# Two multi-head attentions of a gated cross-attention network: loops unrolled, each projection split one and three matmuls, queries and norms on ScalarE

## The reference, cut to what matters

```
scores = q @ k.T            # per head, 256 x 256
w      = softmax(scores)    # A2: masked keys at a huge negative value
heads  = w @ v              # 256 x 16 per head
out    = concat(heads) @ Wo
```

## Time and profile before

| | us |
|---|---|
| runs shown, median (lowest to highest) | 3025.44 (3023.05 to 3033.63) |
| profiled execution, its own time | 3053.3 |
| its span, first to last instruction | 3051.6 |
| MHA window, 190 to 965 us | 775 |
| A2 window, 1778 to 2165 us | 387 |

### The profile page before, as it was taken

How to read it: one execution, slowest core, us unless ns; L and a number is a source line. 1 busy time by engine, 2 the same in 40 slices (tenths; PEclk the granted TensorE clock), 3 DMA queues, 4 the chain that set the end, 5 groups by cost and what they waited for, 6 DMA issues and landing times. The chain is left out here.

```text
span 3051.6 us, 56496 instructions
## 1 busy us (share of the span) xinstructions
PE 2722.6 (89%) x19773; PEld 2165.8 (71%) x19774; DVE 1743.8 (57%) x4748; ACT 1143.3 (37%) x2188; POOL 627.0 (21%) x1027
## 2 busy tenths in 40 slices
PE   7978999989897899899899778888799998978998
PEld 6855666666665788787787645555588887877998
DVE  5757777777775111688675468888422217861111
ACT  1224444444443221454334424444333324452221
POOL 1211212121221000110464511111011104551111
PEclk9989999999998899999789979999799999988999
DMA  9610000000000443670214311000111102025553
GB/s 324 262 33 2 1 1 1 1 1 1 1 1 2 154 152 134 245 285 11 96 69 133 112 52 30 22 22 15 65 56 55 44 12 77 15 93 184 180 181 120
DMA packets 136169, 247.47 MB, mean 81 GB/s; under 512 B 26716, under 2 KB 86364, under 8 KB 129632
## 3 DMA queue, kind: packets, MB, share of 16 engines
q1 hardware_dynamic: 114608, 185.11, 18.0%
q10 hardware_dynamic: 11536, 35.28, 3.0%
q0 software_dynamic: 9888, 25.38, 2.3%
HBM read 148.75 MB, written 97.75 MB: 81 GB/s over the span
## 5 line engine op out<-in xcount | busy, mean ns | idle before, releaser
L564 ACT ACTIVATE m0hpT<-banks 128x1024 f32<-128x1024 f32 x256 | 262.9, 1027 | 415.3 <-PE banks L501 413.8
L539 DVE TENSOR_REDUCE m0hnm<-banks 128x4 f32<-128x1024 f32 x256 | 312.0, 1219 | 158.4 <-PE banks L488 156.9
L488 PE MATMUL banks<-m0hk,m0hq 32*128 32x256 f32 x2048 | 294.9, 406 | 71.4 <-DVE m0hnm L539 69.6
L501 PE MATMUL banks<-m0hq,m0hk 32*128 32x256 f32 x2048 | 294.3, 404 | 1.4 <-ACT m0hpT L564 1.4
L488 PEld LDWEIGHTS banks<-m0hk,m0hq 32*128 32x128 f32 x2048 | 177.4, 187 | 165.0 <-DVE m0hnm L539 142.4
L562 ACT ACTIVATE a2hpT<-banks,a2hlow 128x512 f32<-128x512 f32 x256 | 162.2, 684 | 208.0 <-PE banks L501 208.0
L539 DVE TENSOR_REDUCE a2hnm<-banks 128x4 f32<-128x1024 f32 x128 | 156.5, 1223 | 73.7 <-PE banks L488 73.6
L488 PE MATMUL banks<-a2hk,a2hq 32*128 32x256 f32 x1024 | 148.1, 407 | 44.6 <-DVE a2hnm L539 44.6
L501 PEld LDWEIGHTS banks<-m0hq,m0hk 32*128 32x128 f32 x2048 | 179.7, 186 | 3.2 <-issue 1.5
L488 PEld LDWEIGHTS banks<-a2hk,a2hq 32*128 32x128 f32 x1024 | 88.9, 187 | 98.0 <-DVE a2hnm L539 80.5
L3252 PEld LDWEIGHTS banks<-E3xT,E3w 128*128 128x128 f32 x1248 | 147.3, 194 | 2.4 <-DVE E3xT L3176 0.5
(11 more groups left out here) (492 smaller groups left out, 6219.9 us busy)
## 6 DMA issues: line engine op xcount, KB each, us to landing
E3w<-in_L_ffn_W_dram SPq DMA_DIRECT2D x39, 1024.0 KB, 4.8
slots<-A0pad SPq DMA_DIRECT2D x8, 4290.0 KB, 34.2
slots_x<-A1pad ACTq DMA_DIRECT2D x8, 4290.0 KB, 14.3
E0w<-in_L_ffn_fw_dram SPq DMA_DIRECT2D x64, 512.0 KB
E2w<-in_L_ffn_w_dram SPq DMA_DIRECT2D x16, 1024.0 KB
E1xin<-slots SPq DMA_DIRECT2D x71, 130.0 KB
m0hq<-m0hnmT SPq DMA_DIRECT2D x512, 1.0 KB
A2routed<-routed SPq DMA_DIRECT2D x16, 512.0 KB, 3.6
```

The costliest lines, as they stand in the source:

```text
L488: ins = pe.matmul(self.scores[:, j, tc], self.q[strip(half, j), u, e, c, chunk(tc)], self.k[strip(half, j), u, e, c], start=True, stop=True)
L501: ins = pe.matmul(self.turned[:, j, kc], self.k[strip(half, j), u2, e2, c2, chunk(kc)], self.q[strip(half, j), u2, e2, c2], start=True, st ...
L539: v.tensor_reduce(self.nm[:, e, :, at:at + 9:8].rearrange("p c g -> p g c"), self.scores, AX.X, ALU.max, negate=True).then_inc(self.nm_rdy, 1)
L564: ins = a.activation(dst, self.turned, ACT.Exp)
```

## The change

All loops in the two stages go: every batch is written out, with plain integer numbers. PE's order becomes

```diff
+    def tensor(self, pe, n, one=None, rest=None):
+
+        if self.has(n):
+            self.score(pe, n, 0)
+        if self.has(n - 2):
+            self.score_turned(pe, n - 2, 1)
+        if self.has(n - 3):
+            self.weighted(pe, n - 3)
+        if one:
+            one()
+        if self.has(n):
+            self.score(pe, n, 1)
+        if self.has(n - 2):
+            self.score_turned(pe, n - 2, 0)
+        if rest:
+            rest()
```

and a projection comes in two pieces, where one() is the first of four matmuls:

```diff
+def parted(pe, out, lhsT, rhs, ready, sem, after=None):
+
+
+    order = [(m, k) for m in range(C) for k in range(C)]
+
+    def step(m, k):
+        return pe.matmul(out(m), lhsT(k, m), rhs(k), start=(k == 0), stop=(k == C - 1))
+
+    def one():
+        ready()
+        step(*order[0])
+
+    def rest():
+        for m, k in order[1:]:
+            ins = step(m, k)
+        ins.then_inc(sem, 1)
+        if after:
+            after()
+    return one, rest
```

In MHA each of the eight units has one product; the output product is cut by token chunk, 4 matmuls in unit 4 and 4 in unit 7, and goes to bank 5 instead of bank 7:

```diff
+                    hd.tensor(pe, 8 * b, *make_v(0, ready0, after0))
+                    hd.tensor(pe, 8 * b + 1, *make_qk(wq, 1, G0, q_mm, ready1))
+                    hd.tensor(pe, 8 * b + 2, *make_qk(wk, 1, G1, k_mm, ready2))
+                    hd.tensor(pe, 8 * b + 3, *make_v(1, ready3, after3))
...
+                    hd.tensor(pe, 8 * b + 4, *sum_out(b - 1, 0, ready4, after4))
...
+                    hd.tensor(pe, 8 * b + 5, *make_qk(wq, 0, G0, q_mm, ready5))
+                    hd.tensor(pe, 8 * b + 6, *make_qk(wk, 0, G1, k_mm, ready6))
...
+                    hd.tensor(pe, 8 * b + 7, *sum_out(b - 1, 1, lambda: None, after7))
```

Layer norms: POOL computes from one set of statistics both roots (for the doubled norm by algebra) and a shift, and ACT applies them; the copy keep goes, and POOL recomputes the normalised input for the base with two more tensor_scalar:

```diff
+            def norm1(b):
+                r = b % 4
+                g.wait_ge(st1_rdy, b + 1)
+                g.tensor_scalar(var1[:, r, 1], mv1[:, r, :, 1], 1.0 + 1e-6, 1e-11, ALU.mult, ALU.add)
+                ch1.link(g.tensor_tensor(var1[:, r, 0], mv1[:, r, :, 1], env.eps5[:], ALU.add))
+                ch1.link(g.tensor_tensor(root1[:, r].rearrange("p t c -> p (t c)"), var1[:, r].rearrange("p t c -> p (t c)"),
+                                         env.mhalf[:, 0:2 * C], ALU.pow))
+                for c in range(C):
+                    ins = g.tensor_scalar(shift1[:, r, c:c + 1], mv1[:, r, c, 0:1], root1[:, r, 1, c:c + 1], -1.0,
+                                          ALU.mult, ALU.mult)
+                ins.then_inc(rstd1_rdy, 1)
...
+            def take_q(job, e):
+                a.wait_ge(q_mm, job + 1)
+                for c in range(C):
+                    ins = a.activation(hd.q[:, job % 2, e, c], G0[:, c], ACT.Identity, bias=bqe[:, job % 2, e, c:c + 1],
+                                       scale=hd.column(2 + e))
+                if e == 1:
+                    ins.then_inc(hd.q_rdy, 1)
+
...
+            def apply1(b):
+                a.wait_ge(rstd1_rdy, b + 1)
+                if b:
+                    a.wait_ge(n1_mm, b)
+                for c in range(C):
+                    ins = a.activation(nn1[:, c], env.x[:, b, c], ACT.Identity, scale=root1[:, b % 4, 1, c:c + 1],
+                                       bias=shift1[:, b % 4, c:c + 1])
+                ins.then_inc(nn1_rdy, 1)
```

```diff
+            def add_routed(b):
+
+                g.wait_ge(high_in[b % 2], 16 * (b // 2 + 1))
+                g.tensor_tensor(env.x[:, b], env.x[:, b], routed[:, b % 2, :, 0:D], ALU.add).then_inc(high_add, 1)
+                g.wait_ge(high_add, b + 1)
+                g.tensor_tensor(env.x[:, b], env.x[:, b], routed[:, b % 2, :, D:2 * D], ALU.add).then_inc(low_add, 1)
...
+            def add_bias(b):
+
+                g.wait_ge(xn_rdy, b + 1)
+                g.tensor_tensor(env.x[:, b], env.x[:, b], bp[:].unsqueeze(1).broadcast_to([P, C, D]), ALU.add).then_inc(bias_rdy, 1)
...
+            def finish(b):
+                v.wait_ge(bias_rdy, b + 1)
                 v.wait_ge(y_mm, b + 1)
-                v.tensor_tensor(y[:], G1, bp[:].unsqueeze(1).broadcast_to([P, C, D]), ALU.add).then_inc(y_rdy, 1)
-
-            def finish(b):
-                v.wait_ge(y_rdy, b + 1)
-                v.scalar_tensor_tensor(env.x[:, b], y[:], env.tg[:, 2:3], env.x[:, b], ALU.mult, ALU.add)
-
-            ch.start(0)
...
+                def pre3():
                     if more:
+                        take_k(b + 1, 0)
...
+                hd.tensor(pe, 4 * b, one0, rest0)
+                if more:
+                    hd.tensor(pe, 4 * b + 1, *make_q(b + 1, ready1))
+                    hd.tensor(pe, 4 * b + 2, *make_k(b + 1, ready2))
+                    hd.tensor(pe, 4 * b + 3, *make_v(b + 1, ready3))
```

More of the change, by code:

```diff
@@ L532, in vector, with has @@
-    def vector(self, v, job, u, i, first, mid=None, end=None):
-        new = self.parts(i, first)[0]
-        n, _, c, e = self.unit(job, u, i)
-        def highest(half):
-            v.wait_ge(self.s_mm, 2 * n + half + 1)
-            at = 16 * half
-            v.tensor_reduce(self.nm[:, e, :, at:at + 9:8].rearrange("p c g -> p g c"), self.scores, AX.X, ALU.max,
-                            negate=True).then_inc(self.nm_rdy, 1)
-        if new:
-            highest(0)
+    def has(self, n):
+        return 0 <= n < self.units
@@ new lines, in weighted @@
+    def weighted(self, pe, n):
+        u, c, e = self.place(n)
+        if n % 4 == 0:
+            pe.wait_ge(self.v_rdy, n // 4 + 1)
+        if e == 0 and n:
+            pe.wait_ge(self.raw_rdy, n // 2)
+        pe.wait_ge(self.p_rdy, 2 * n + 2)
+        for kc in range(C):
+            for g in range(4):
+                ins = pe.matmul(self.out[32 * g:32 * g + 32, e], self.v[:, u, kc, 8 * c + 2 * g + e],
+                                self.pT[:, e, g, kc], start=(kc == 0), stop=(kc == C - 1), tile_position=(0, 32 * g))
+        ins.then_inc(self.av_mm, 1)
@@ L953, in _, with rows_of @@
         @block.scalar
         def _(a):
-            def turned(mm, count, bank, dst, gain, bias, sums, done, at):
+            def rows_of(mm, count, dst, gain, bias, sums, done, at):
                 a.wait_ge(mm, count)
@@ L2272, in job @@
-            def job(b, u, first, last):
-                start, more = first and u == 0, not (last and u == 1)
-                ch.start(b + 2)
+            first_stats(0)
+            last_stats(0)
+            take_k(0, 0)
+            take_k(0, 1)
+            first_stats(1)
+            last_stats(1)
+            add_flags(1, 5).then_inc(low_rdy, 1)
+            v.wait_ge(low_rdy, 2)
+            v.wait_ge(hd.made, 3)
+            for b in range(B + 2):
+                more = b + 1 < B
                 def end0():
-                    if not start:
+                    if within(b - 1):
@@ L2386, in _ @@
+            one()
+            rest()
             turn(0, G1)
-            pe.wait_ge(q_in, 16)
-            make_q(0)
-            pe.wait_ge(w_in, 16 * loads)
-            make_v(0)
-            def job(b, u, first, last):
-                start, more = first and u == 0, not (last and u == 1)
-                def fill0():
+            pe.wait_ge(xnT_rdy, 1)
+            one, rest = make_q(0, lambda: pe.wait_ge(q_in, 16))
+            one()
+            rest()
+            pe.wait_ge(hd.q_rdy, 1)
```

1088 lines of the change are left out of this document (509 added, 579 removed).

## The result

The changed kernel takes 2914.36 us, median of 4 runs (2908.54 to 2917.27), the one before 3024.24 (3022.89 to 3033.63) on the same chip: a ratio of 0.9628, 95% interval 0.9603 to 0.9653. The profiled execution took 2908.5 us, its span 2906.7.

The account below looks back on a forecast made before the run. No engine full; order bounds: PE and DVE take turns in phase A (half 0 to half 1), PE sets phase B (the rest of a unit). MHA 67 and A2 33 us, together 100 off 3025.4: 2925 us, range 2880 to 2975.

Parts of the forecast that it names:

- Unit: One group of heads with two maxima: PE's work 2.63 us in phase A, 2.55 in phase B, together 5.18.
- Turns and logits: Extra PE work in MHA, two of each per batch, four at 0.50 us on top of eight units.
- DVE's lateness: MHA maxima held up: 0.3 us a batch by DVE's own work plus 0.4 by POOL, 0.7 in all.
- The collision of DVE and POOL: MHA unit 3's residual add, both inputs in SBUF, beside POOL's base: 0 to 0.9 us a batch, taken as 0.4.
- The rival of 2983 us: DVE's two-input adds wait up to 1.27 us behind POOL, six places, 58 us more in all; chance 0.12.
- DVE gives work away: Per MHA batch DVE loses four query takes and all normalisation applications; the second statistics go altogether.
- A2's batch: Units of 5.8, 5.18, 5.18 and 5.75 us, sum 21.9, saving 2.1 a batch; unit 3's maximum 0.6 late.
- The rival of code loading: Straight-line PE code must stream, from 5 us per former loop pass; at 6 us the time is 3045; chance 0.04.
- Start and tail: MHA starts 2 us earlier; its tail ends 2 to 3 later, as batch 14's second norm moves behind the last scores.
- Full drains: Rival: each unit's two new shape changes cost 0.14 us more, 27 us over 192 units: 2952; chance 0.15.
- Overlap: Rival: PE's shape changes overlap, the unit falls to 5.0 us, 35 us more gained: 2890; chance 0.12.
- no change: Rival: the single matmul delays half 1 as much as phase B shortens, DVE stays late: 3025; chance 0.03.

Follow-up runs that it names:

- experiment 1: Changed kernel with the single matmul put back, products whole behind half 1's scores, MHA's output product still halved: 2952.52 us, ratio 0.9765.
- experiment 2: Changed kernel with queries and norm applications back on DVE in both stages, PE's new order kept: 2944.32 us, ratio 0.9732.
- experiment 5: Changed kernel with MHA's output product in one piece in unit 4, none in unit 7: 2941.80 us, ratio 0.9732.
- experiment 6: Changed kernel with A2's two adds of routed rows on DVE again instead of POOL: 2934.30 us, ratio 0.9686.
- experiment 8: Changed kernel with the single matmul ahead of the weighted sums instead of behind them: 2918.82 us, ratio 0.9655.
- experiment 10: Changed kernel with four parts undone at once, those of experiments 1, 2, 5 and 6: 2997.66 us, ratio 0.9908.
- experiment 3: Changed kernel with the edits of experiments 1 and 2 together: 2978.97 us, ratio 0.9839.
- experiment 11: Kernel of experiment 10 with A2's last statistics and residual also back behind unit 1's second maximum: 3007.95 us, ratio 0.9936.
- experiment 4: Kernel before the change with its loops over batches written out, nothing else: 3024.62 us, ratio 0.9988.
- experiment 9: Changed kernel with router's logits in phase A and the product whole behind half 1, in MHA units 0 and 7: 2920.10 us, ratio 0.9634.

## Why the prediction was right, step by step

**The time and the cause** held: PE's gaps in phase A and its surplus in phase B, both set by DVE, are gone, and the two stages are 112 us shorter, against 100 forecast. PE's new order alone carries a third of it (experiment 1), DVE's relief, the halved output product and A2's adds the larger part (experiments 2, 5 and 6), and some 20 us are placed in no part. What each part brought came out otherwise than the terms had it.

**Unit, 5.18 forecast, 5.30 measured.** The mis-sized term is the single matmul. I took a record's step as the mean over a whole product, (1.99 - 0.38)/7 = 0.23 us. The first step of a group is 0.32 and the others 0.215, so the mean holds for no part of it: two records cost 0.62 instead of 0.54, six 1.49 instead of 1.46 us (experiment 8). The step from weighted sums to the full shape, which no row showed and for which I took 0.31, came out as taken (1.01 against 1.00). A plain unit then was said to fall from 5.56 to 5.18; experiment 1 shows 5.48 to 5.30. The split fills a gap of 0.37 us (5.48 - 5.11, the sum of PE's work unsplit) and costs 0.19 (5.30 - 5.11). A third of the gain, where my unit gave it over half.

**Turns and logits, 2.0 a batch forecast, 1.56 measured.** Behind a product they need no change of shape: by the phases 0.34, 0.50, 0.37, 0.34. **DVE's lateness, 0.7 forecast, about 0.1 measured** (units 2 and 6: 5.35 and 5.36). The three errors cancel: 8 x 5.30 + 1.56 + 0.1 = 44.06, for 44.1 forecast. That agreement is luck.

**The collision of DVE and POOL, 0.4 a batch, did not come in the changed kernel.** The residual and POOL's first operation of the base, in the trace of the changed kernel:

```profile
510.49 2.09 POOL L738 TENSOR_SCALAR M0shift<-M0bo,M0probs 128x256 f32<-128x256 f32 x2
```

```profile
511.08 0.71 DVE L801 SCALAR_TENSOR_TENSOR x_all<-M0x,tg,x_all 128x512 f32<-128x512 f32 x1
```

DVE's addition with both inputs in SBUF followed its transposition without a gap and ran inside POOL's pair, in 0.71 us. By the Trainium skill's rule that I weighed (SBUF — State Buffer, Who interferes with whom) DVE would have waited for the end of POOL's operation; this row does not show that. POOL's pair took 2.09 us, where it took 1.83 in experiment 10. The rival of 2983 us falls for this kernel. But the rival had a true core, in another place: DVE's norm from SBUF to SBUF took 2.25 us beside both of POOL's additions in experiment 3, and 1.17 us where it overlapped only the first. By giving the norms to ACT the change took that operation off DVE.

**ACT's cost nothing** held: its exponentials are released by PE. **DVE gives work away** had no number of its own; experiment 2 gives 30 us in the median and, of 22 in the profile, 21 in MHA. **A2's batch** was 21.9 for 21.82, by compensation: units 1 and 2 took 5.37 and 5.62 instead of 5.18, unit 3 5.06 instead of 5.75. The key take makes a maximum 0.3 late, not 0.6, which the timeline puts at the end of unit 2, and the following phase A recovers 0.24 of it. The part that I had named in a clause (adds, statistics and finish behind one maximum) is the largest of A2: experiments 6 and 11.

**Unrolling** cost nothing: over the whole of MHA's batch 1 there are 4 instruction packets on that queue in both kernels (the 3 of the earlier trace rows leave out the batch's first 0.2 us), PE has no idle time there that is put down to issue, and experiment 4 finds 0.9988. The rival of code loading falls. **Start and tail:** the first maximum came 2.5 us earlier (forecast 2), but it moves by as much from run to run (188.0 and 190.6 us with the same MHA code); from the last maximum to the last pick 33.1 us instead of 32.9, not 2 to 3 longer. **Full drains** (2952) put 0.14 on a unit; 0.12 was measured, but from the second record on. So in size that rival was nearly right on the unit; what I had priced too dear elsewhere made up for it. The Trainium skill (TensorEngine Tiling (Array Packing), Key Properties) says that a change of tiling mode drains the engine; the runs put the price of one more change at 0.19 us (experiments 1 and 9), and whether a drain is what takes it none of them shows. **Overlap** (2890) and **no change** fall with the same rows.

## What to carry over

Two engines that take turns on the same banks waste the difference of their phases; a split of a product pays only if the gap that it fills (0.37 us here) is wider than the change of shape that it adds (0.19), and so one matmul ahead pays where two do not. Small work on the pacing engine is priced by place: 1.4 us in a middle slot of its own cost nothing, in a slot with other work 0.45, and 1.0 to 1.4 us behind a maximum 0.6 to 0.8. A record is priced by its position in its group and not by the group's mean. And parts are undone both alone and together: the output product and the adds were worth 27 and 20 us alone, and 19 for both with the other parts gone. An undone part can also bring a cost of its own, as DVE's norm beside POOL does.

## What the runs showed of the hardware that was not expected

A group of matmuls of a new shape starts slowly twice: 0.31 us to its first record and 0.32 to its second, then 0.215 (128x256 fp32, both with the weighted sums and with scores ahead). The granted clock can fall to 0.50 right behind two idle stretches of 0.31 and 0.85 us (PE busy 2.15 of the 3.00 us ahead); each fall lasted 3.4 us and cost about 1.7, or 0.9 us a batch (experiment 5). The rule of the Trainium skill (TensorE: Matmul & The Clock Gate, Part 1: The HAM clock gate), by which the clock follows PE's recent activity, fits that; in the changed kernel, where PE has no gap, it stayed at 1.00 for 613 us. But the same stretches came without a fall in every second batch and in experiment 10, so they alone don't decide it.

A DVE operation with both ends in SBUF can be held up by POOL. Two TENSOR_SCALAR of 128x256 took 0.73 us at the start of MHA and 2.25 beside POOL's two TENSOR_TENSOR, ending 0.15 us after the second of them (experiment 3). A SCALAR_TENSOR_TENSOR of 128x512 beside POOL's TENSOR_SCALAR kept its 0.71 us, and POOL's pair took 2.09 instead of 1.83.
